# Decoder kernel on one Trainium2 core: output projection and layer norm in one stage per tile; recurrence, gate and quantized network from another version

## The reference

```
x = x + L0_attn(norm(x));  x = x + L0_xattn(ctx, norm(x));  x = x + L0_ffn(norm(x))
x = x + L1_attn(norm(x));  x = x + L1_xattn(norm(x), ctx);  x = x + L1_ffn(norm(x))
x = x + L2_attn(norm(x));  x = x + L2_xattn(norm(x), ctx);  x = x + L2_ffn(norm(x))
x = x + L3_attn(norm(x));  x = x + L3_xattn(norm(x), ctx);  x = x + L3_ffn(norm(x))
norm(x) = (x - mean) / sqrt(var + 1e-5)
```

```
L1_attn:  r, k, v = split(x @ W + b);  r = sigmoid(r);  k = exp(k)
          u1, u2 = running sums over time of k*v and k with decay lam
          out = ((u1 + gamma*k*v) / (u2 + gamma*k + 1e-6) * r) @ W_o + b_o
L3_attn:  y = mish(h @ wg) * group_norm(retention(h)) @ wo + x;  mish(g) = g * tanh(softplus(g))
          out = gelu(norm2(y) @ w1 + b1) @ w2 + b2 + y
L3_ffn:   h = silu(conv3(quant(x) @ quant(w1).T));  out = quant(h) @ quant(w2).T
          quant(x) = clip(round(x * s), -128, 127) / s,  s = 127 / max|row|
```

## Time and profile before

| | us |
|---|---|
| median of 3 runs | 2572.27 (2570.31 to 2578.26) |
| profiled execution, whole | 2567.72 |
| its span of instructions | 2565.8 |
| PE busy | 1868.0 (73%) |
| DVE busy | 1474.4 (57%) |
| ACT busy | 1006.5 (39%) |
| POOL busy | 834.5 (33%) |

### The profile page before, as it was taken

The page is one execution under the profiler, slowest core; times in us unless marked ns, Lnnn a source line. Parts: engine busy times, 40 slices in busy tenths (PEclk is TensorE's granted clock), DMA queues, the critical chain, the costliest instruction groups (busy, mean ns, idle before and its releaser), DMA issues. The chain is left out here.

```text
span 2565.8 us, 32196 instructions
## 1 busy us (share of the span) xinstructions
PE 1868.0 (73%) x11486; PEld 939.6 (37%) x11509; DVE 1474.4 (57%) x2552; ACT 1006.5 (39%) x1598; POOL 834.5 (33%) x734
## 2 busy tenths in 40 slices
PE   4685969999755767666746785999665737799834
PEld 2343422222533444445633551333244325222223
DVE  2544244441474898983244446999434563677476
ACT  2252114444212454451323331888622213266634
POOL 1000024444012999992121031666532203000014
PEclk8897979999777898986878898999978868699966
DMA  4611461110009106003215425321232102623000
GB/s 160 144 38 38 154 198 58 58 34 8 17 16 203 45 14 96 1 2 116 87 58 162 135 94 132 71 55 36 99 116 85 39 0 76 168 54 80 9 1 17
DMA packets 165904, 190.64 MB, mean 74 GB/s; under 512 B 14516, under 2 KB 132350, under 8 KB 164710
## 3 DMA queue, kind: packets, MB, share of 16 engines
q1 hardware_dynamic: 162676, 180.20, 25.5%
q0 software_dynamic: 3072, 8.39, 1.0%
HBM read 124.17 MB, written 68.30 MB: 75 GB/s over the span
## 5 line engine op out<-in xcount | busy, mean ns | idle before, releaser
L2675 POOL TENSOR_TENSOR a2x_masked<-a2x_masked,tall_rows 128x512 f32<-128x512 f32 x128 | 163.3, 1276 | 116.6 <-ACT a2x_masked L2638 116.6
L1130 ACT ACTIVATE experts<-a1x_scores 128x1024 f32<-128x1024 f32 x128 | 124.0, 1021 | 176.6 <-PE a1x_scores L1061 176.6
L2686 DVE TENSOR_REDUCE a3x_row_most<-a3x_ring 128x1 f32<-128x512 f32 x256 | 159.3, 682 | 51.8 <-PE a3x_ring L2534 51.8
L741 DVE TENSOR_REDUCE a0x_row_most<-a0x_rows 128x2 f32<-128x1024 f32 x88 | 107.8, 1225 | 139.0 <-PE a0x_rows L584 139.0
L2686 DVE TENSOR_REDUCE a2x_row_most<-a2x_ring 128x1 f32<-128x512 f32 x256 | 162.2, 679 | 18.0 <-DMA k_scr<-p2x_hml 16.6
L566 POOL TENSOR_TENSOR a0x_pair_sums<-a0x_probs_T 128x1024 f32<-128x1024 f32 x48 | 113.0, 2353 | 164.9 <-ACT a0x_probs_T L688 164.9
L1166 POOL TENSOR_TENSOR a1x_tree<-experts 128x1024 f32<-128x1024 f32 x64 | 150.3, 2349 | 42.2 <-ACT experts L1130 42.0
L1099 DVE TENSOR_TENSOR experts<-experts,a1x_inverse_total 128x2048 f32<-128x2048 f32 x64 | 145.7, 2276 | 4.2 <-ACT a1x_inverse_total L1143 4.2
L1050 PE MATMUL a1x_scores<-a1x_qs,a1x_ks 96*128 96x128 bf16 x1024 | 91.8, 243 | 72.1 <-ACT experts L1130 45.8
L2631 ACT ACTIVATE a3x_probs_T<-a3x_scores_T 128x1024 f32<-128x1024 f32 x128 | 123.2, 1018 | 47.5 <-PE a3x_scores_T L2561 47.5
L2631 ACT ACTIVATE wide_rows<-a2x_masked 128x1024 f32<-128x1024 f32 x128 | 135.9, 1062 | 1.6 <-POOL a2x_masked L2675 1.4
(11 more groups left out here) (653 smaller groups left out, 4290.3 us busy)
## 6 DMA issues: line engine op xcount, KB each, us to landing
v_scr<-p0x_vout SPq DMA_DIRECT2D x24, 256.0 KB, 2.0
k_scr<-p0x_x SPq DMA_DIRECT2D x24, 256.0 KB, 2.0
a0x_ks<-k_scr SPq DMA_DIRECT2D x8, 768.0 KB, 4.9
a0x_vs<-v_scr SPq DMA_DIRECT2D x8, 768.0 KB, 5.4
experts<-in_L_ffn_w SPq DMA_DIRECT2D x8, 768.0 KB, 7.0
v_scr<-p1x_vout SPq DMA_DIRECT2D x16, 256.0 KB, 2.1
a1x_vs<-v_scr SPq DMA_DIRECT2D x16, 256.0 KB, 8.7
v_scr<-p2x_vout SPq DMA_DIRECT2D x16, 256.0 KB, 2.2
```

The lines of the kernel that those rows point to most:

```text
L741: nc.vector.tensor_reduce(rm[:, qt, :, c], row_psum(r)[:, :, :], AX.X, ALU.max).then_inc(row_most, 1)
L1130: nc.scalar.activation(ex[:, n % E, 8 * half:8 * half + 8, :], sp_[:, g % 3, :, :, :].rearrange("p i j q -> p (i j) q"), ACT.Exp).then_inc ...
L2675: nc.gpsimd.tensor_tensor(sm[:, i % 2, 1, :], sm[:, i % 2, 1, :], full[1][:, i // 2 % KT, :], ALU.add).then_inc(pool_masked, 1)
L2686: nc.vector.tensor_reduce(rm[:, u % 2, h * QT + qt:h * QT + qt + 1, part], ring[:, row_place(r) % 3, 0:n], AX.X, ALU.max).then_inc(row_mos ...
```

## The change

Ten calls of `out_stage` become `out_norm_stage`, which also makes the norm behind it, and the ten `norm_stage` calls go (ln0x, ln0f, ln1a, ln1x, ln1f, ln2x, ln2f, ln3c, ln3x, ln3f). Two of the ten (o0a, o3x) need no turned copy. The three loads of expert weights that ln1f started are now started by the router stage behind it. The recurrence, the gate and both quantized stages are rewritten too.

The core of the diff, in the order of the file:

```diff
-def out_stage(core, name, src, w, addends=(), dst=None, row_scale=None, turned_src=False, loads=(), far=()):
+def out_norm_stage(core, name, src, w, normed, normed_T, nw=None, nb=None, addends=(), dst=None, row_scale=None,
+                   turned_src=False, loads=(), far=()):
...
             @block.gpsimd
             def _(pool):
+                nc.gpsimd.memset(eps[:, :], EPS).then_inc(eps_set, 1)
...
+                def turn_normed(t):
+                    pe.wait_ge(xn_done, t + 1)
+                    if t >= 2:
+                        pe.wait_ge(xn_moved, t - 1)
+                    for k in range(KH):
+                        mm = nc.tensor.transpose(np_[:, t % 2, k * P:(k + 1) * P], normed[:, t, k * P:(k + 1) * P],
+                                                 core.ident[:, :])
+                    mm.then_inc(xn_turned, 1)
...
                     mm.then_inc(product, 1)
+                    if normed_T is not None and t >= 3:
+                        turn_normed(t - 3)
+                if normed_T is not None:
+                    for t in range(NT - 3, NT):
+                        turn_normed(t)
+            @block.scalar
+            def _(act):
...
+                act.wait_ge(eps_set, 1)
+                nc.scalar.activation(first_root[:, :], eps[:, 0:1], ACT.Sqrt)
+                if not turned_src:
+                    move(0)
+                for s in range(NT + 3):
+                    if not turned_src and s + 1 < NT:
+                        move(s + 1)
+                    if s < NT:
+                        root(s)
+                    if 1 <= s <= NT:
+                        normalize(s - 1)
+                    if s >= 3 and normed_T is not None:
+                        move_normed(s - 3)
             @block.vector
             def _(dve):
-                for t in range(NT):
+                def add(t):
...
                     nc.vector.tensor_tensor(dst[:, t, :], dst[:, t, :], term, ALU.add).then_inc(added, 1)
+                    dve.wait_ge(added, t + 1)
+                    nc.vector.bn_stats(stats[:, t, :], dst[:, t, :]).then_inc(stat, 1)
...
+                for t in range(NT):
+                    add(t)
+                    aggregate(t)
+                    if t >= 1:
+                        inverses(t - 1)
+                inverses(NT - 1)
 def recurrence_stage(core, name, w, xT, outT, loads=()):
...
+                def invert(i):
+                    act.wait_ge(denom, i + 1)
+                    nc.scalar.activation(den[:, i % 2, :], den[:, i % 2, :], ACT.Ln).then_inc(logged, 1)
+                    act.wait_ge(logged, i + 1)
+                    nc.scalar.activation(inv[:, i % 2, :], den[:, i % 2, :], ACT.Exp, scale=-1.0).then_inc(inverse, 1)
+                nc.scalar.preload_act_table_set("natural_log_exp_and_others")
...
+                inputs(0)
+                for i in range(1, len(jobs)):
+                    if i == 1:
+                        inputs(1)
+                    invert(i - 1)
+                    if i + 1 < len(jobs):
+                        inputs(i + 1)
+                invert(len(jobs) - 1)
+            @block.gpsimd
+            def _(pool):
...
+                weigh(0)
+                weigh(1)
+                for i in range(len(jobs)):
+                    finish_job(i)
+                    if i + 2 < len(jobs):
+                        weigh(i + 2)
...
-                    nc.vector.tensor_tensor(kv_, k_, v_, ALU.mult).then_inc(step, 1)
...
-                    nc.vector.reciprocal(v_, v_).then_inc(step, 1)
-                    dve.wait_ge(step, n + 8)
-                    nc.vector.tensor_tensor(out, kv_, v_, ALU.mult).then_inc(step, 1)
 def gate_stage(core, name, xT, wg, retT, bm, yT, loads=()):
...
+                for u in range(U):
+                    pool.wait_ge(numer, u + 1)
+                    pool.wait_ge(affine, u + 1)
+                    nc.gpsimd.tensor_tensor(out_of(u), nn[:, u, :], out_of(u), ALU.mult).then_inc(weighted, 1)
...
-                    nc.vector.reciprocal(rn[:, s, :], rn[:, s, :]).then_inc(step, 1)
...
+                def invert(u):
+                    act.wait_ge(numer, u + 1)
+                    nc.scalar.activation(rn[:, u, :], nn[:, u, :], ACT.Ln, bias=two[:, 0:1]).then_inc(logged, 1)
+                    act.wait_ge(logged, u + 1)
+                    nc.scalar.activation(rn[:, u, :], rn[:, u, :], ACT.Exp, scale=-1.0).then_inc(inverse, 1)
...
 def bit_in_stage(core, name, xn, w1q, mean1, hT, loads=()):
...
-        jobs = [(f, b) for f in range(F) for b in range(B)]
+        jobs = [(f, b) for b in range(B) for f in range(F)]
...
+                for i in range(1, len(jobs), 2):
+                    f, b = jobs[i]
+                    pool.wait_ge(scaled, i + 1)
+                    if i >= 2:
+                        pool.wait_ge(silued, i - 1)
+                    nc.gpsimd.tensor_tensor(side[:, :], hp[:, i % R, 2:T + 2], cw[:, 2, f:f + 1].to_broadcast([P, T]),
+                                            ALU.mult).then_inc(pool_conv, 1)
+                    pool.wait_ge(pool_conv, i)
+                    pool.wait_ge(conv, taps(i + 1))
+                    nc.gpsimd.tensor_tensor(side[:, :], side[:, :], cv[:, i % R, :], ALU.add).then_inc(pool_conv, 1)
...
 def bit_out_stage(core, name, hT, w2q, mean2, loads=()):
...
+                for t in range(NT):
+                    if t + 1 < NT:
+                        scales(t + 1)
+                    clip(t)
+                    if t >= 2:
+                        add(t - 2)
...
-                for t in range(NT):
-                    pool.wait_ge(step, 4 * (t + 1))
-                    nc.gpsimd.tensor_scalar(rounded[:, t % 3, :], rounded[:, t % 3, :], ROUND - 128, ROUND + 127,
-                                            ALU.max, ALU.min).then_inc(clipped, 1)
...
+                def round_up(t):
+                    act.wait_ge(scale_step, 3 * (t + 1))
+                    if t >= 3:
+                        act.wait_ge(whole, t - 2)
+                    nc.scalar.activation(rounded[:, t % 3, :], hp[:, t % 2, :], ACT.Identity, bias=whole_by[:, 0:1],
+                                         scale=scale[:, t:t + 1]).then_inc(rounds, 1)
...
```

427 lines of the change are left out of this document (265 added, 162 removed).

## The result

The changed kernel takes 2512.64 us (median of 4 runs, 2510.55 to 2515.78), the one before 2571.73 on the same chip: a ratio of 0.9766, 95% interval 0.9752 to 0.978, 59.1 us less. The forecast was 2502 us and a range of 2478 to 2525, so direction and range were right and the gain was a sixth smaller than forecast. In the profiled executions the span went from 2565.8 to 2512.0, 53.8 less, where my sum said 70.5.

What follows compares the result with a forecast made beforehand. No engine is busy over 73% of the span, so the chain that ends each stage sets the time. Gains of 20 + 17 + 23.5 + 4.5 + 5.5 = 70.5 us from 2572.3 give 2502 us, range 2478 to 2525.

Steps and rivals of the forecast that it cites:

- fused stages: Ten output projections with their norms: a shorter tail behind the last addition, less pace lost ahead of it, wins 20 us.
- recurrence: DVE loses the reciprocal and two products per job; the stage wins 17 us, between 13 and 20.
- gate: The same trade on four units, with ACT inverting beside clamps and numerators; wins 23.5 us, between 20 and 25.
- bit_in: Quantized stage: pipeline starts 2.4 us earlier, a pair of jobs costs 3.4 to 3.9; wins 4.5 us, between 0 and 8.
- bit_out: Last stage: POOL's 3.62 us clip goes, tiles take 3.45 instead of 3.97; wins 5.5 us, between 2 and 9.
- the round trip: Rival: o2a's wait of ACT's moves on DVE's statistics paces all ten fused stages, which win nothing: 2522 us; chance 0.11.
- The step that failed: Costing method: only stages the change touches are costed, each from its first instruction to the first of the next.
- the granted clock among the rivals: Stages meet PE at its high clock as the norms' idle stretches go; 12 us more won, 2490 us; chance 0.16.
- The rival: POOL and DVE slow each other on 512 columns, 0.2 us on 40 operations; 8 us fewer won, 2510; chance 0.11.
- The low clock as slower case: Rival: PE drops to its low level in the fused stages and stays; 2588 us, slower than before; chance 0.03.
- a drain behind a table load: A skill page's 1.38 us after each ACT table load: four stages start later, sum 5.5 us smaller; chance 0.03.
- The signs it named: Expected stage lengths and addition spacings; wrong if turned-stage additions exceed 1.7 apart, o0x-to-o3x clock nears 0.5, POOL products exceed 1.6.

Runs made afterwards that it cites:

- e5: The changed kernel, but in the four fused stages that turn their source ACT moves the source two tiles ahead instead of one; 2502.43 us.
- e8: The kernel before with only the ten fused stages changed; recurrence, gate and both quantized stages as before; 2561.84 us, ratio 0.9962.
- e9: The kernel before with only the ten fused stages changed, plus needless PE turns in their tails; 2547.7 us, ratio 0.99.
- e4: The changed kernel, with PE turning the identity into an unused bank while it waits in the fused tails; 2497.69 us, ratio 0.9715.
- e1: The changed kernel, but with both plain products of each recurrence job on DVE instead of POOL; 2515.5 us, ratio 0.9783.
- e6: The changed kernel, but in bit_in DVE makes both side taps of every job and POOL makes none; 2517.76 us, ratio 0.9802.
- e10: The changed kernel with the edits of e4, e5, e1 and e6 in one; 2489.7 us, ratio 0.9688.
- e7: The kernel before the change, with 20 needless POOL products of 128 x 512 added through the recurrence; ratio 1.0047.
- e2: The changed kernel with the bit_in stage of the kernel before put back; 2516.78 us, ratio 0.9787.

## Why the prediction was right, and where it was wrong

The sum, term by term: 70.5 forecast; fused stages +5.2, recurrence -5.9, gate -0.6, bit_in -7.0, bit_out +2.9, untouched stages -11.3; 53.8 measured in the profiled spans.

Terms that came out better (8.1) and terms that came out worse (24.8) offset each other in part, so the total is nearer to the forecast than the terms are. That much is luck.

**Fused stages, 20 forecast, 25.2 by their own length.** Right in mechanism and a little small in size. The tail of 4.3 was exact, the pace 1.30 instead of 1.4 in turned stages, and 1.89 instead of 1.87 in o2a, by the round trip that e5 then took away. o0x won 5.7 and o1x 5.6 (4.6 forecast), o1a 4.9 (3.9), o3b 5.3 (4.3), o3a 3.5 (1.5), o0f 1.5 (0.9), o2a and o2x 0.6 each (0.2); o0a and o3x with their norms lost 2.5 (0.5). The three moved loads of experts cost nothing that can be seen: m1f took 147.1 for 146.3.

**The step that failed: "each stage that the change touches is costed from its first instruction to the first of the next".** That priced the stages behind at nothing. Alone, the fused stages moved the kernel by 9.6 us (e8), and by 22.5 with PE kept busy (e9). I had the granted clock among the rivals, with the opposite sign: I took the removed idle of 6.3 us ahead of the turns as a gain for the clock. Inside the fused stages it was one: o0x went from a mean of 0.77 to 0.91, o1a from 0.70 to 0.89, o2a from 0.77 to 0.82. But right ahead of the next stage fusing took work from PE (at p2x 3.07 of 4 us before, 1.07 after), and e4 and e9 show that giving it work there gives the next stage the high level. The profile of before hinted at it: p1x and p2x began at the high level right behind a row of turns. The recurrence did not, so the rows alone gave no rule, and its 2.1 us in e4 are a new gain, not one given back.

**Recurrence, 17 forecast, 11.1 measured.** The trade of the reciprocal for ACT's logarithm and exponential was right; the term was mis-sized by the hold-up between POOL and DVE. The rival had the cause and put it at 0.2 us on 40 operations; measured, it is mostly 0.7 to 1.1 per instruction. The Trainium skill, "SBUF — State Buffer", section "SBUF: two separate sides", describes the port pair that the two share as an exclusive lock, held for a whole instruction, where the loser blocks fully. The trace agrees: the DVE steps that wait for POOL in this stage end 0.28 to 0.55 behind POOL's end, and the products on PSUM (L2460) stay at 0.68 beside POOL. In stage lengths the hold-up cost 2.7 here (e1), 3.5 in bit_in (e6) and about 0.6 in the gate, 6.8 together. So the rival's 8 us were near the truth by luck: more per instruction than I said, on fewer of them. Without POOL the stage wins 13.8 (e1), and 15.4 with PE at its high level as well (30.5 in e10); the last 1.6 of the 17 stay open.

**Gate, 23.5 forecast, 22.9 measured.** Right; DVE's last product of a unit takes up to 1.75 beside POOL. That of the third unit takes 1.34 at 2052.92, that of the fourth, without POOL, 0.69: the 0.65 between them stand just ahead of the stage's last two steps and account for the 0.6.

**bit_in, 4.5 forecast, 2.5 lost.** Both steps failed. The pair of jobs takes 4.19 us (2457.24 to 2461.43 and on), not 3.4 to 3.9, and without POOL 4.09 (e6): POOL's tap relieved DVE of nothing, and its addition and a silu at the end were pure cost. And the first tap comes 0.3 us earlier, not 2.4.

**bit_out, 5.5 forecast, 8.4 measured.** The pace was right (maxima of tiles two apart come 6.71 us apart, forecast 6.9), but the clock of the first 16 us was 0.74, not the 0.50 for which I took off 1.5.

**Rivals.** The round trip paces the stages that turn their source and no others. The low clock as slower case (0.03) had the right agent in the wrong place: the mean in the fused stages was 0.79 to 0.91, and it is the start of the stage behind that is hit. No run here shows a drain behind a table load: in o2a the load ends at 1463.80 and the root begins at 1463.81.

**The signs it named.** Additions of turned stages are 1.30 apart and the fused stages' clock is far from 0.5, as it should be. But four of POOL's eight products in the recurrence took over 1.6 (1.76 to 2.07), which the prediction called a sign of being wrong, and it was: for that stage's term. The lengths are 15.8 for o1a with its norm (16.8 forecast), 34.8 for the recurrence (29), 18.8 for the gate (18), and 32.5 from the last stage's first instruction to the end of its last addition (35).

## What to carry to other kernels

When a stage is made shorter or smoother, look at what PE did in the last microseconds before the next one starts, and at that one's first: a shorter tail with an idle PE cost the next stages here some 10 of the 25 us won, and a few needless transposes won about as much. Don't move an elementwise step from DVE to POOL where both read SBUF at the same time without counting what it adds on DVE: here mostly 0.7 to 1.1 us for each DVE instruction that met one of POOL's. Where an engine serves two chains in one loop, order its list so that the move another engine waits for doesn't stand behind a wait for that engine's result.

## What was new about the hardware

- A DVE instruction that begins while one of POOL's runs ends only after POOL's, at most its own length later (0.28 to 0.55 us later for instructions of 0.40 to 0.75). This holds also for a DVE `tensor_scalar` of one SBUF input (0.40 us alone, 1.44 beside POOL) and for scans (1.22 to 2.05); a reciprocal (3.35) and a product that reads PSUM (0.68) are free of it. In e7 ten POOL products lengthened a DVE job from 9.33 to 15.6 us.
- Needless PE work made the kernel 13 to 15 us faster (e4), of which 9.1 stand in the stages right behind it. The stages' first 4 us went from a granted 0.50 to 0.62 to 1.00, with PE busy 2.67 instead of 1.07 us in the 4 us ahead of p2x.
- The granted clock at the start of an unchanged stage differs from run to run: ctxT's first 8 us had 0.80, 1.00, 0.81 and 0.66 in four kernels with the same o0a ahead of it (the changed one, e1, e2, e6). What decides between them isn't shown.
